# Attention denominators from sums over four key tiles, a third score bank, and moved projection and scaling steps, in a conditioned transformer block on one core

## What is computed

```python
def _tc_rmsnorm(x, t, gw, gb, bw, bb):
    g = (t @ gw.T + gb)[:, None, :]
    b = (t @ bw.T + bb)[:, None, :]
    return g * x * rsqrt(mean(x * x) + EPS) + b
# 16 heads of 32
attn = einsum('blhd,bmhd->bhlm', q, k) / scale
o = einsum('bhlm,bmhd->blhd', softmax(attn), v)
x1 = x + o @ Wo.T
y = x1 + (silu(n(x1) @ gate.T) * (n(x1) @ hid.T)) @ out.T
out = x + y
```

## Time and profile before

| | |
|---|---|
| median of 3 runs | 2507.95 us (2507.72 to 2508.66) |
| profiled execution | 2508.16 us |
| its span in the trace | 2506.1 us |
| PE, DVE, ACT, POOL busy share | 95%, 66%, 52%, 46% |
| one batch (start of one L503 to the same in the next batch) | 489.64 to 844.20 us: 354.56 us |

### The profile page before, as it was taken

The page is one execution under the profiler, slowest core; times in us unless marked ns, Lnnn a source line. Parts: engine busy times, 40 slices in busy tenths (PEclk is TensorE's granted clock), DMA queues, the critical chain, the costliest instruction groups (busy, mean ns, idle before and its releaser), DMA issues. The chain is left out here.

```text
span 2506.1 us, 39896 instructions
## 1 busy us (share of the span) xinstructions
PE 2375.7 (95%) x11396; PEld 1578.2 (63%) x11396; DVE 1661.6 (66%) x2732; ACT 1308.1 (52%) x2287; POOL 1145.1 (46%) x1095
## 2 busy tenths in 40 slices
PE   5999999999999999999999957999999999999999
PEld 4655436554447554456544436888888888888887
DVE  4766735666725666527667436887688778877877
ACT  3366762566762556743667724446344544454454
POOL 0265661456650565532556634641473157216711
PEclk8999999999999999999999978999999999999999
DMA  5212203212122122132122053115411541254125
GB/s 191 66 40 61 58 22 107 50 40 68 47 71 66 35 68 50 48 94 51 39 55 57 30 168 126 60 55 168 166 55 60 180 151 52 68 169 152 51 77 175
DMA packets 92670, 209.75 MB, mean 84 GB/s; under 512 B 15632, under 2 KB 15632, under 8 KB 90640
## 3 DMA queue, kind: packets, MB, share of 16 engines
q1 hardware_dynamic: 91344, 202.71, 27.1%
q0 software_dynamic: 1088, 4.19, 0.5%
HBM read 134.23 MB, written 19.92 MB: 62 GB/s over the span
## 5 line engine op out<-in xcount | busy, mean ns | idle before, releaser
L418 POOL TENSOR_TENSOR sums<-probs 128x512 f32<-128x512 f32 x512 | 648.4, 1292 | 708.2 <-ACT probs L567 706.7
L641 DVE TENSOR_REDUCE pmax<-bank 128x1 f32<-128x512 f32 x1024 | 654.2, 684 | 280.6 <-PE bank L854 272.5
L567 ACT ACTIVATE probs<-bank 128x512 f32<-128x512 f32 x1024 | 584.7, 597 | 371.6 <-PE bank L938 338.6
L938 PE MATMUL bank<-qs,ks 128*128 128x512 f32 x1024 | 458.6, 452 | 28.5 <-ACT probs L567 27.8
L938 PEld LDWEIGHTS bank<-qs,ks 128*128 128x128 f32 x1024 | 190.9, 187 | 372.0 <-ACT probs L567 226.6
L854 PE MATMUL bank<-ks,qs 96*128 96x512 f32 x1024 | 398.1, 401 | 4.0 <-DVE pmax L641 3.6
L1501 PE MATMUL bank<-H_hi,wt_hi 128*128 128x512 f32 x896 | 349.9, 390 | 14.6 <-DVE H_lo L1356 14.6
L1515 PE MATMUL bank<-ow,aw 128*128 128x512 f32 x1536 | 358.7, 392 | 0.0
L1501 PE MATMUL bank<-H_lo,wt_hi 128*128 128x512 f32 x896 | 349.5, 390 | 0.0
L1501 PE MATMUL bank<-H_hi,wt_lo 128*128 128x512 f32 x896 | 349.5, 390 | 0.0
L1515 PEld LDWEIGHTS bank<-ow,aw 128*128 128x128 f32 x1536 | 285.6, 188 | 59.9 <-issue 1.2
(11 more groups left out here) (136 smaller groups left out, 3139.1 us busy)
## 6 DMA issues: line engine op xcount, KB each, us to landing
raw<-in_gu_w SPq DMA_DIRECT2D x66, 512.0 KB, 3.6
wo_raw<-in_out_w SPq DMA_DIRECT2D x128, 256.0 KB, 2.6
ks<-qk_hi SPq DMA_DIRECT2D x136, 128.0 KB, 2.4
qs<-qk_hi SPq DMA_DIRECT2D x264, 64.0 KB, 2.0
x<-in_x SPq DMA_DIRECT2D x10, 1024.0 KB, 5.1
ks<-qk_lo SPq DMA_DIRECT2D x68, 128.0 KB, 2.4
qs<-qk_lo SPq DMA_DIRECT2D x132, 64.0 KB, 2.0
wv<-wv_parts SPq DMA_DIRECT2D x4, 2048.0 KB, 9.1
```

The source lines that it names most:

```text
L418: nc.gpsimd.tensor_tensor(sums[:, h, :], probs[:, 0, h, :], probs[:, 1, h, :], ALU.add) \
L567: nc.scalar.activation(probs[:, s % 2, h, :], sbank[i % SB][:], ACT.Exp, scale=SCALE).then_inc(st_done, 1)
L641: nc.vector.reduce_max(pmax[:, t, h, hf:hf + 1], mbank[n % MB][:], AX_X).then_inc(sq_done, 1)
L938: nc.tensor.matmul(sbank[i % SB][:], ks[:, g % 2, h, s * P:(s + 1) * P], qs[:, u % 3, h, :], start=True, stop=True).then_inc(st_ready, 1)
```

## The change

- Denominators: POOL now sums four key tiles (a quad) before PE multiplies by `ones`. 3 adds per head and quad, 24 in a unit in place of 16. PE makes 2 groups of four matmuls in a unit in place of 4, at (5, 1) for key tiles 0 to 3 and at (1, 1) of the next unit for 4 to 7 (`SUMS_AT`). They go to the work bank as tiles ("D", u, 0) and ("D", u, 1), each started afresh: ACT copies the first to `den`, DVE adds the second to it.
- The denominators' bank becomes a third score bank: SB = 3.
- `values` is at h = 3, 1, 3, 2 for s % 4 = 0, 1, 2, 3; the copy of a finished unit's output is at (0, 3) in place of (1, 0).
- Q projections of a unit's head have gap 1 in place of 2, some K projections too; `HT_AT` and the last K of a batch move.
- The scaling of the next batch's tokens goes from DVE to ACT (same places).
- At the batch's end the last denominators come after the second output tile, and DVE empties the first output tile before it.

```diff
-PAIRS = 4
+QUADS = 2
+QT = 4
 for odd in (1, 3):
-    PROJECTED.update({("Q", odd + 2): (odd * UNIT, 2), ("K", odd + 3, 0): (odd * UNIT + 18, 2),
+    PROJECTED.update({("Q", odd + 2): (odd * UNIT, 1), ("K", odd + 3, 0): (odd * UNIT + 14, 1),
                       ("K", odd + 3, 1): ((odd + 1) * UNIT, 1), ("Q", odd + 3): ((odd + 1) * UNIT + 9, 2)})
-PROJECTED.update({("Q", NU - 1): (5 * UNIT, 2), ("Q", NU): (6 * UNIT, 2), ("K", NU, 0): (7 * UNIT + 16, 2),
-                  ("K", NU, 1): (7 * UNIT + 24, 2)})
-HT_AT = {5: (10, 14, 18, 22), 7: (0, 4, 8, 12)}
+PROJECTED.update({("Q", NU - 1): (5 * UNIT, 1), ("Q", NU): (6 * UNIT + 8, 2), ("K", NU, 0): (7 * UNIT + 8, 1),
+                  ("K", NU, 1): (7 * UNIT + 26, 1)})
+HT_AT = {5: (9, 13, 17, 24), 7: (13, 16, 19, 23)}
+SUMS_AT = {(5, 1): (0, 0), (1, 1): (1, 1)}
+VALUES_AT = (3, 1, 3, 2)
-SB, MB = 2, 3
+SB, MB = 3, 3
-    obank, dbank, wbank = psum[5], psum[6], psum[7]
+    obank, wbank = psum[6], psum[7]
 # gpsimd
-                        for h in range(GH if s % 2 else 0):
+                        for h in range(GH if s % QT else 0):
                             pool.wait_ge(st_done, SCORES_T(b, NT + n * GH + h + 1) + SB)
-                            if h == 0:
-                                pool.wait_ge(d_ready, products_done(b, u, s // 2))
-                            nc.gpsimd.tensor_tensor(sums[:, h, :], probs[:, 0, h, :], probs[:, 1, h, :], ALU.add) \
+                            if s % QT == 1 and h == 0:
+                                pool.wait_ge(w_ready, MISC(b, sums_before(u, s // QT)))
+                            if s % QT > 1:
+                                pool.wait_ge(sum_done, sums_done(b, u, s - 1, h))
+                            first = probs[:, 0, h, :] if s % QT == 1 else sums[:, h, :]
+                            nc.gpsimd.tensor_tensor(sums[:, h, :], first, probs[:, s % 2, h, :], ALU.add) \
                                 .then_inc(sum_done, 1)
 # scalar
+            def scale_x(b, hf, t):
+                act.wait_ge(inv_ready, b * 2 + 3 + hf)
+                nc.scalar.activation(x4[:, t, :], x4[:, t, :], ACT.Copy, scale=inv[:, t:t + 1]).then_inc(x_scaled, 1)
+                elif tile[0] == "D":
+                    u = tile[1]
+                    act.wait_ge(on_done, b * NU + (u + 1))
+                    nc.scalar.activation(den[:], bank[:], ACT.Copy).then_inc(w_act, 1)
-                            if s % 2 == 0:
-                                act.wait_ge(sum_done, sums_done(b, u, s // 2 - 1, h) if s
-                                            else sums_done(b, u - 1, PAIRS - 1, h))
+                            if s % QT != QT - 1:
+                                act.wait_ge(sum_done, sums_done(b, u, s - 2, h) if s >= 2
+                                            else sums_done(b, u - 1, NS + s - 2, h))
+                            if (s, h) == (5, 2):
+                                work_tile(b, ("D", u, 0))
-                            if (s, h) == (1, 0) and u:
+                            if (s, h) == (0, GH - 1) and u:
                                 output(b, u - 1)
-                            if (s, h) == (1, 2) and u:
-                                denominators(b, u - 1)
 # vector
+                elif tile[0] == "D":
+                    nc.vector.tensor_tensor(den[:], bank[:], den[:], ALU.add).then_inc(w_dve, 1)
 # tensor
+            def denominators(b, u, quad):
+                work_bank_empty(b, ("D", u, quad))
+                pe.wait_ge(sum_done, sums_done(b, u, QT * quad + QT - 1, GH - 1))
                 for h in range(GH):
-                    last = nc.tensor.matmul(dbank[DH * h:DH * h + DH, :], ones[:], sums[:, h, :], start=(pair == 0),
-                                            stop=(pair == PAIRS - 1))
-                last.then_inc(d_ready, 1)
+                    last = nc.tensor.matmul(wbank[DH * h:DH * h + DH, :], ones[:], sums[:, h, :], start=True, stop=True)
+                last.then_inc(w_ready, 1)
-                            if h == 2 + (s + 1) % 2 and (u or s):
+                            if h == VALUES_AT[s % QT] and (u or s):
                                 values(b, u if s else u - 1, (s - 1) % NS)
-                                if s % 2 == 0:
-                                    denominators(b, u if s else u - 1, (s // 2 - 1) % PAIRS)
+                            if sums_at(u, s, h):
+                                denominators(b, *sums_at(u, s, h)[1:])
```

More of the change, by code:

```diff
@@ L89, in misc_order @@
     return list(IN_V.values()) + [tile for u in range(NU) for s in range(NS) for h in range(GH)
-                                    for tile in done_at(u, s, h)]
+                                    for tile in done_at(u, s, h)] + [("D", NU - 1, 1)]
 def part_at(u, s, h):
@@ L105, in made_at, with sums_at @@
     return ("mT", u + 1) if (s, h) == MAXIMA_AT and u < NU - 1 else None
+def sums_at(u, s, h):
+    back, quad = SUMS_AT.get((s, h), (NU, 0))
+    return ("D", u - back, quad) if u >= back else None
 def next_maxima(u, s, h):
@@ L116, in done_at, with act_reads, dve_reads @@
     tile, part = part_at(u, s, h) or (None, 0)
-    return [m for m in (made_at(u, s, h), tile if part == KT - 1 else None) if m]
+    return [m for m in (made_at(u, s, h), tile if part == KT - 1 else None, sums_at(u, s, h)) if m]
+def act_reads(tile):
+    return (tile[0], tile[-1]) != ("D", 1)
+def dve_reads(tile):
+    return tile[0] != "mT" and (tile[0], tile[-1]) != ("D", 0)
 LEAD_MISC = misc_order(False)
@@ L122 @@
 MISC = Counter(len(LEAD_MISC), len(BODY_MISC))
-LEAD_DVE = [m for m in LEAD_MISC if m[0] != "mT"]
-BODY_DVE = [m for m in BODY_MISC if m[0] != "mT"]
+MISC_ACT = Counter(sum(map(act_reads, LEAD_MISC)), sum(map(act_reads, BODY_MISC)))
+LEAD_DVE = [m for m in LEAD_MISC if dve_reads(m)]
+BODY_DVE = [m for m in BODY_MISC if dve_reads(m)]
 MISC_DVE = Counter(len(LEAD_DVE), len(BODY_DVE))
@@ L130 @@
 SCORES_Q = Counter(0, NU * NMAX + NT)
[L131 to L132 removed]
+SUMS = QUADS * (QT - 1) * GH
+assert QT * QUADS == NS
 LINKS_PER_BATCH = NU * (2 + 2)
@@ L138, in misc_index, with sums_before @@
     return (BODY_MISC if body else LEAD_MISC).index(tile)
+def sums_before(u, quad):
+    if quad:
+        return misc_index(True, ("D", u, 0)) + 1
+    return misc_index(True, ("D", u - 1, 1)) + 1 if u else 0
 def slot_users(tile):
@@ L152, in qk_slot, with sums_done, act_before @@
     return tile[2] if tile[0] == "K" else 0
[L155 to L162, removed]
+def sums_done(b, u, s, h):
+    return b * (NU * SUMS) + (SUMS * (u + 1) + GH * (s // QT * (QT - 1) + max(s % QT, 1) - 1) + h + 1)
+def act_before(body, tile):
+    order = BODY_MISC if body else LEAD_MISC
+    return sum(map(act_reads, order[:order.index(tile)]))
 def dve_before(body, tile):
     order = BODY_MISC if body else LEAD_MISC
-    return sum(m[0] != "mT" for m in order[:order.index(tile)])
+    return sum(map(dve_reads, order[:order.index(tile)]))
 def hold(sp, held, semaphore, value):
@@ L365, in _ @@
                 hold(sp, held, pv_done, b * (NU * NS) + NU * NS + 2)
-                hold(sp, held, sum_done, sums_done(b, NU - 1, PAIRS - 1, GH - 1))
+                hold(sp, held, sum_done, sums_done(b, NU - 1, NS - 1, GH - 1))
                 load_wv()
@@ L623, in work_tile @@
                 dve.wait_ge(w_ready, MISC(b, misc_index(body, tile) + 1))
-                dve.wait_ge(w_act, MISC(b, misc_index(body, tile) + 1))
+                if act_reads(tile):
+                    dve.wait_ge(w_act, MISC_ACT(b, act_before(body, tile) + 1))
                 bank = wbank if body else lead_bank(misc_index(body, tile))
@@ L750, in _ @@
                                 max_tile(b, NMAX + n)
[L751 to L754, removed]
                             for tile in done_at(u, s, h):
-                                if tile[0] != "mT":
+                                if dve_reads(tile):
                                     work_tile(b, tile)
@@ L774, in out_tile @@
                     nc.vector.tensor_copy(yout[:, t % 2, :], mbank[n % MB][:]).then_inc(sq_done, 1)
-                for t in range(3):
+                for t in range(2):
                     lo_part(t)
+                out_tile(0)
+                for t in range(2, 4):
+                    lo_part(t)
+                work_tile(b, ("D", NU - 1, 1))
                 for part in range(3):
                     normalise(b, NU - 1, part)
-                for t in range(NT):
+                for t in range(1, NT):
                     out_tile(t)
@@ L806, in work_bank_empty @@
                 if b is not None:
-                    pe.wait_ge(w_act, MISC(b, i))
+                    pe.wait_ge(w_act, MISC_ACT(b, act_before(True, tile)))
                     pe.wait_ge(w_dve, MISC_DVE(b, dve_before(True, tile)))
@@ L959, in _ @@
                              lambda c, k: wo[c][:, k, :], NG, sq_ready)
-                    if t == 0:
-                        denominators(b, NU - 1, PAIRS - 1)
```

(2 more changed lines are left out.)

36 lines of the change are left out of this document (15 added, 21 removed).

## The result

The changed kernel takes 2483.6 us in the median of 4 runs (2478.29 to 2487.19), against 2508.3 us before (2507.72 to 2508.98): a ratio of 0.9902, 95% interval 0.9887 to 0.9917. It is faster by 24.7 us where 84 were forecast, and lies outside the range of 2390 to 2468. In the later jobs the kernel before took 2506.1 to 2508.2 us in the median, and its own runs spread over 8 us, as those of the changed kernel do here, so a difference of 2 us between jobs says nothing. One execution of run 8 (4463.95 us) and one of the kernel before in its job (2681.53 us) are in the slow state and left out of every comparison.

The account below looks back on a forecast made before the run. PE's time, with stalls on ACT, was taken as the bound. Between -13.8 us a batch (products only) and -33 (POOL-PE floor) it took -21, four times -84, giving 2424 us, range 2390 to 2468.

Parts of the forecast that it names:

- Products, -55 us: Denominators on PE: 16 groups fewer a batch at 0.86 us each, 13.8 us a batch, -55 us over four.
- Stalls between POOL, PE and ACT: Units' quads: POOL and PE equal at about 16.2 us, some PE stalls staying; no lag closing a shorter circle.
- Third bank: Score banks in the units: usual 0.15 us holds go, removing about half of 30 us of stalls, cut short by POOL's floor.
- the 7 net that the forecast took: Gain per batch beyond the products' 13.8 us, from 19 us between the ends, after the scaling and unit 7's gain.
- Adds on POOL: 24 adds a unit, 1.24 us apart: 14.9 us per quad, 16.2 with the passage to PE.
- rival 3: POOL becomes the bound with adds costing more than now: 2536 us at 1.45 us each, 2600 at 1.53; chance 0.06.
- Scaling on ACT: Token scaling at (4, 6) and (6, 7), 8 instructions of some 0.5 us: costs 1 us a batch, bounds 0 and 4.
- Unit 7: Last unit of a batch, already about at POOL's new pace: gains little, taken as 1 us.
- End of batch: Output tiles and last denominators: costed at nothing, with bounds of +2 and -2 us.
- Rival 1: Only the products go, stalls handed back: -13.8 us a batch less up to 3 returned, 2453 to 2465 us; chance 0.25.

Follow-up runs that it names:

- run 8: Changed kernel with token scaling on VectorE, unit 7's transposed tiles at heads 0, 8, 12, 16 and its K projections later: 2485.88 us, ratio 0.9916.
- run 10: Changed kernel with the values of each unit's first key tile made twice, 32 more groups ahead of the second denominators product: 2512.88 us, ratio 1.0022.
- Runs 4: Changed kernel with a second sums buffer for the second quad in units 0 to 2: 2465.38 us, ratio 0.9821.
- run 6: Changed kernel with the four first adds of each quad covering 16 of 512 columns, the eight later ones full: 2440.7 us, ratio 0.9732.
- run 2: Changed kernel with two score banks, the third lying idle: 2497.77 us, ratio 0.9964.
- run 3: Changed kernel with the adds of each quad's third and fourth key tile covering 16 of 512 columns: 2473.7 us, ratio 0.9858.
- run 1: Changed kernel with the token scaling back on VectorE: 2470.6 us, ratio 0.9852.
- run 11: Kernel before the change with only the token scaling moved to ScalarE: 2527.24 us, ratio 1.0074.

## Why the forecast was wrong, point by point

*Products, -55 us: right.* PE's busy time fell by 66 us, and 32 groups put back cost 29.3 us (run 10), so 64 removed are worth some 55 to 59.

*Stalls between POOL, PE and ACT: the step that failed first.* The forecast said "I find no place where the lag closes a circle shorter than 16.2 us", put this term at nothing, and treated POOL and PE as two loops of equal length of which the longer counts. Their lengths were about right, 14.9 us for 12 adds and 16.2 for a quad of PE. But with one buffer they depend on each other *within* the quad: product, then 5.0 us of first adds, and only with these the exponentials of the key tile after, at 1.24 us each where three banks hold scores for three heads. PE stalls then, comes late to the next product, and POOL waits for it. Two quads took 34.9 us in place of 32.4. Runs 4 and 6 give 33.0 as soon as that link is cut, so it costs 2 us in a plain unit.

The sum then about closes. The forecast gave units 0 to 6 some 18 of its 21 us a batch; they gained 9.4. In run 6, without the link, they take 235.3 us on average, 18.0 less than the 253.3 before. So products and third bank together are worth about what was forecast there, and the link took 8.6 us a batch of it back.

Before the change a product stood at (s, 3), one head ahead of the first add that had to wait for it; now it stands at (5, 1) and (1, 1), one head behind. This fits with the rows of before, in which POOL's adds wait for ACT and not for PE, but no run puts the product back one head ahead.

*Third bank.* It is worth 5.6 us a batch in units 0 to 6 (run 2), of the 7 net that the forecast took; over the whole run it is 14 us in place of 28, as unit 7 is longer with it.

*Adds on POOL:* 1.24 us apart and 1.28 long, as forecast; rival 3 did not come about. The slow case stayed where it had been, in the last four adds of unit 7, first before, then after:

```profile
734.13 5.99 POOL L418 TENSOR_TENSOR sums<-probs 128x512 f32<-128x512 f32 x4 [3.30 <-ACT probs L567]
727.66 5.92 POOL L447 TENSOR_TENSOR sums<-sums,probs 128x512 f32<-128x512 f32 x4 [0.16 <-ACT probs L599]
```

The number of later adds was beside the point (run 3).

*Scaling on ACT, 1 us a batch, 4 as the upper bound: mis-sized.* It measures 3.3 us a batch (run 1), within the bound, and 4.9 in the kernel before (run 11). The duration was taken from the square's start-to-start distance of 0.5; the scaling takes 0.71 us (0.61 from start to start), it meets two copies of maxima, and a lower clock follows, which the forecast didn't count at all.

*Unit 7, a gain of 1 us a batch beside its products: wrong in sign.* It lost 3.5 on average, of which run 1 gives 2.9 back. Why it gains nothing from its missing products even there is open: POOL is busy 36.51 of its 38.67 us then, but no run had both the scaling on VectorE and shorter adds.

*End of batch at nothing:* +0.1 us in the second batch, right there; the other batches moved by +1.3 and -2.5.

Rival 1 had the mechanism in outline, "a wait on POOL takes the place of that on ACT", but priced what is handed back at up to 3 us a batch; with unit 7 it was 7.6.

## What to carry to other kernels

Where two engines pass one buffer back and forth, adding up each one's work isn't enough: follow what the first item behind the hand-over releases, and ask whether a third engine waits for it. Four short items there brought 2 us a unit here, eight short ones later none. And an engine with half its time free can still be the wrong place for 4 instructions, if they fall where it already has a burst.

## What the runs showed that was not expected

The granted clock fell to 0.50 in the 5 us after PE had been busy 2.49 of 5.00 us, so a short burst on ACT can cost more than its own length. In the kernel before, 32 scalings of 0.71 us (23 us of ACT's time in all, on an engine that is idle almost half of the span) made the whole 19.4 us slower. Batches of one execution differ, too: unit 7 took 39.6 to 43.2 us in the changed kernel, and the lower its clock the longer it took.

The scaling is not free on VectorE either, beside POOL's adds. In the kernel before POOL stood idle for most of them; in run 1 it is adding all the while. Four scalings of the same unit 6, first before, then in run 1:

```profile
695.78 1.67 DVE L618 TENSOR_SCALAR x<-x,inv 128x512 f32<-128x512 f32 x4 [1.64 <-POOL inv L390]
676.45 5.74 DVE L650 TENSOR_SCALAR x<-x,inv 128x512 f32<-128x512 f32 x4 [2.79 <-POOL inv L415]
676.38 10.63 POOL L447 TENSOR_TENSOR sums<-sums,probs 128x512 f32<-128x512 f32 x8
```

The median of one over the batches rose from 0.48 to 1.47 us, and the eight adds beside them took 10.63 us where the same eight took 9.87 in the changed kernel. VectorE had the time: unit 6 was 0.6 us shorter all the same. No run moves these scalings away from the adds, so the overlap as the cause is a reading of the rows.
